# First layer's self-attention by pairs of heads: two heads' scores side by side in two row groups, eight steps, division one step later

## The chip, the cores and the metric

The kernel runs on one core of one Trainium2 chip. The metric is the device time of one execution in microseconds (us), the median of several. The core has a matrix engine (TensorE, PE in the profile), whose weight loads are shown apart (PEld), a vector engine (VectorE, DVE), an activation engine (ScalarE, ACT), GpSimd (POOL) and SyncE (SP), which issues most DMAs. Each engine runs its own list of instructions in order; semaphores tie the lists together. TensorE reads from SBUF (here one big tensor, `arena`) and writes to PSUM, which has eight banks of 128 partitions x 512 f32 words.

## The reference

Two decoder layers over 4 sequences of 512 tokens with 256 features. The first layer has a Mamba block with a grouped-query attention and a gated feed-forward inside it, a cross-attention with 16 heads, and a mixture of experts. The second has block-diagonal attention, cross-attention and another mixture of experts. The change touches only this part of the first layer:

```python
N_HEADS = 4
N_KV = 2
head_dim = D // N_HEADS          # 64
q = (xn @ q_w.T).reshape(B, L, N_HEADS, head_dim).transpose(0, 2, 1, 3)
k = (xn @ k_w.T).reshape(B, L, N_KV, head_dim).transpose(0, 2, 1, 3)
v = (xn @ v_w.T).reshape(B, L, N_KV, head_dim).transpose(0, 2, 1, 3)
k = jnp.repeat(k, hpg, axis=1)   # hpg = 2: heads 0, 1 use key head 0, heads 2, 3 key head 1
v = jnp.repeat(v, hpg, axis=1)
attn = jnp.einsum('bhqd,bhkd->bhqk', q, k) * scale
attn = jnp.where(causal[None, None], -jnp.inf, attn)
attn = jax.nn.softmax(attn, axis=-1)
out = jnp.einsum('bhqk,bhkd->bhqd', attn, v)
out = out.transpose(0, 2, 1, 3).reshape(B, L, D) @ o_w.T
```

## The kernel before, in words

The program is written out by hand, engine by engine: the order on each engine is the order of the source, and every wait names a semaphore and a count. The first layer runs one sequence after the other (the loop over `b`, four rounds). A round is: the selective scan, the output projection of the Mamba block, the self-attention, its output projection, the gated feed-forward, the cross-attention. TensorE takes part in all of them.

The stage that the change touches is the self-attention of a round. It has 16 units `u`, one for each block of 128 queries (`qc = u // 4`) and head (`h = u % 4`). Keys are causal, so block `qc` looks at `nk = 128, 256, 384 or 512` keys. All data are f32. The steps of a unit are:

- `scores(u)` on TensorE (L854, L856): queries x keys of one head into PSUM bank 4 or 5 (by turns). The contraction is over the 64 features of a head, so only 64 of the 128 rows of the array hold weights: rows 0 to 63 for heads 0 and 1, rows 64 to 127 for heads 2 and 3. Then one small bf16 matmul over all 128 rows (L856) adds the causal mask to the last 128 columns.
- `row_max(u)` on VectorE (L2007): minus the maximum of each row.
- the exponential on ScalarE (L1584), with the row sums, which it reads out in a second instruction (ACTIVATION_READ_ACCUMULATOR) before it signals `p_ready`.
- `transpose_p(u)` on TensorE (L863): `qc + 1` transposes into bank 6 or 7, and a copy of them to SBUF by VectorE (L2020).
- `weigh_v(u)` on TensorE (through the helper `acc`, L652, shape 128x64): transposed probabilities x values, into bank 2 or 3.
- after the fourth head of a block: VectorE inverts the four row sums (L2025) and multiplies (L2030, "the division"); TensorE transposes the result (`transpose_o`, L879), ScalarE drains it (L1576).

TensorE's list puts `scores(u + 1)` ahead of `transpose_p(u)`, and `weigh_v(u - 1)` behind it. Between them stand five tiles of the value projection for the cross-attention (`values_tile`, L652, shape 128x512, after the units in `XV_WHEN`); ScalarE drains them (L1571). The tiles go round through PSUM banks 0 and 1, in the order that `XV_AT` and `OT0_AT` number. VectorE's list has `row_max(u + 1)` ahead of the copy of unit `u`; its division of a block stands directly behind the copy of the block's last unit, and waits for that unit's `weigh_v`.

The cross-attention of the same kernel already computes two heads at once: in `xscores` (L938) a loop over two row groups issues one matmul with its weights in rows 0 to 63 and one with rows 64 to 127, next to each other, each 512 columns wide, into two banks.

Of the kernel before, what the change touches and what calls it, by code (L numbers as in the profile page):

```python
# [6 lines left out]
B, L, D = 4, 512, 256  # L7
P = 128
T = B * L
KD = D // P  # L10
NC = L // P
# [11 lines left out]
XV_WHEN, OT0_AT, XK = (1, 3, 5, 9, 13), (3, 5, 7, 8), ("xk_a", "xk_b")  # L23
XV_AT = [("att", i) for i in (0, 1, 2, 4, 6)] + [("xv", i) for i in range(3)]
# [124 lines left out]
def decoder_program(nc, A, out):  # L149
# [5 lines left out]
    with ctx:  # L155
# [48 lines left out]
        caus16 = take16(P)  # L204
# [35 lines left out]
        pr = [take(L) for _ in range(2)]  # L240
        ptb = [take(NC, P) for _ in range(2)]
# [15 lines left out]
        t2 = [take(2, L, at=squares_at + 2 * i * L) for i in range(TBUFS)]  # L257
        sums_at = squares_at + 2 * TBUFS * L
# [387 lines left out]
        def _(pe):  # L646
# [106 lines left out]
            for b in range(B):  # L753
# [94 lines left out]
                def scores(u):  # L848
                    qc, h = u // 4, u % 4
                    nk, g = (qc + 1) * P, h // 2  # L850
                    if u >= 2:
                        w(p_ready, u - 1)
                    s = bank[4 + u % 2]
                    mm(s[:, 0:nk], qT[64 * g:64 * g + 64, h % 2, qc * P:(qc + 1) * P],  # L854
                       kT[64 * g:64 * g + 64, 0:nk], start=True, stop=False)
                    mm(s[:, qc * P:nk], ident16, caus16, start=False, stop=True).then_inc(s_full.sem, 1)  # L856

                def transpose_p(u):
                    w(p_ready, u + 1)
                    if u >= 2:  # L860
                        w(pt_sb, u - 1)
                    for kc in range(u // 4 + 1):
                        r = transpose(bank[6 + u % 2][:, kc * P:(kc + 1) * P], pr[u % 2][:, kc * P:(kc + 1) * P], ident)  # L863
                    r.then_inc(pt_full.sem, 1)

                def weigh_v(u):
                    qc, h = u // 4, u % 4
                    w(pt_sb, u + 1)
                    if h == 0 and qc >= 2:
                        w(o_step, 2 * (qc - 1))  # L870
                    acc(bank[2 + qc % 2][:, 64 * h:64 * h + 64],
                        [(ptb[u % 2][:, kc, :], va[:, kc, 64 * (h // 2):64 * (h // 2) + 64]) for kc in range(qc + 1)])\
                        .then_inc(pv_done.sem, 1)
# [9 lines left out]
                for u in range(U0):  # L883
                    if u + 1 < U0:
                        scores(u + 1)
# [1768 lines left out]
```

## Time and profile before

| | |
|---|---|
| median of 3 runs | 2936.61 us (2935.52 to 2940.99) |
| the profiled execution | 2925.96 us, its span 2924.1 us |
| mean granted TensorE clock of it | 0.945 |
| TensorE busy | 2613.8 us (89% of the span) |
| VectorE busy | 1442.7 us (49%) |
| ScalarE busy | 1088.5 us (37%) |
| GpSimd busy | 681.2 us (23%) |

All durations below are from the profiled execution, which was 10.65 us faster than the median. In the rows, PE MATMUL is a matmul and PEld its weight load. An f32 matmul shows as two MATMUL and two LDWEIGHTS instructions. The ends of matmuls are modelled, and they overlap; what a matmul costs TensorE is read from one start to the next. A row of the timeline merges neighbours and names the first one's shape: the six matmuls at 622.60 are one value product of 64 columns (two) and a value tile of 512 columns (four).

### The profile page before, as it was taken

The numbers are of one execution on the slowest core, as the hardware profiler recorded it, in microseconds if no ns is written. First come the engines' busy times: TensorE is split into PE (matmuls) and PEld (weight loads), VectorE is DVE, ScalarE is ACT, GpSimd is POOL, SyncE is SP. The second block draws the span as 40 slices with busy tenths as digits, with TensorE's granted clock in tenths as the row PEclk, the third lists the DMA queues.
The fourth block names the chain that finished last, engine by engine and source line by source line (L and its number), as shares of the span: only waits on it lengthen the run. The fifth ranks groups of instructions, "written<-read, shape, count | busy, mean of one in ns | idle before, by whom it ended". The sixth has DMA issues, their size and how long they took to land. (4 is left out here: it accounts for less than half of the span.)

```text
span 2924.1 us, 40088 instructions
## 1 busy us (share of the span) xinstructions
PE 2613.8 (89%) x16441; PEld 1564.8 (54%) x16441; DVE 1442.7 (49%) x2107; ACT 1088.5 (37%) x1885; POOL 681.2 (23%) x364
## 2 busy tenths in 40 slices
PE   7679999989999999999949978999989998699997
PEld 4256533844266534754228855464554544477776
DVE  5566337932876347932821124555445554633432
ACT  3764234722564245622502213534335342011111
POOL 0256024900665034900720020000000000022222
PEclk9889999999999999999979987999999998699999
DMA  5550002100030002100039940010100102144442
GB/s 198 200 186 25 0 1 98 60 1 1 1 134 23 1 0 111 46 1 0 1 133 329 343 144 16 1 23 23 22 23 1 23 8 94 34 146 147 166 164 73
DMA packets 62126, 219.25 MB, mean 75 GB/s; under 512 B 12293, under 2 KB 28122, under 8 KB 45178
## 3 DMA queue, kind: packets, MB, share of 16 engines
q1 hardware_dynamic: 45802, 187.39, 17.7%
q0 software_dynamic: 9568, 18.75, 2.7%
q10 hardware_dynamic: 6576, 10.57, 1.0%
q8 instruction: 130, 2.13, 0.3%
q14 instruction: 50, 0.41, 0.0%
HBM read 172.50 MB, written 39.99 MB: 73 GB/s over the span
## 5 line engine op out<-in xcount | busy, mean ns | idle before, releaser
L652 PE MATMUL psum<-arena 128*128 128x256 f32 (+7 forms) x4224 | 1098.4, 411 | 66.4 <-ACT arena L1514 11.5
L652 PEld LDWEIGHTS psum<-arena 128*128 128x128 f32 (+1 forms) x4224 | 679.0, 196 | 434.9 <-issue 321.1
L2473 POOL TENSOR_TENSOR arena<-arena 128x1024 f32<-128x1024 f32 x128 | 299.5, 2372 | 98.4 <-DVE arena L1979 83.5
L1979 DVE TENSOR_TENSOR_SCAN arena<-arena,psum 128x512 f32<-128x512 f32 x256 | 290.8, 1200 | 22.4 <-PE psum L793 14.6
L793 PEld LDWEIGHTS psum<-arena 128*128 128x128 f32 x2048 | 236.6, 193 | 49.4 <-ACT arena L1544 40.3
L793 PE MATMUL psum<-arena 128*128 128x128 f32 x2048 | 249.0, 279 | 2.0 <-issue 1.9
L2508 POOL DMA_INDIRECT arena<-xn,arena x32 | 31.6, 987 | 859.3 <-DVE arena L2415 807.6
L2480 POOL TENSOR_TENSOR arena<-arena 128x1024 f32<-128x1024 f32 x32 | 75.9, 2373 | 653.0 <-ACT arena L1632 653.0
L2073 DVE SCALAR_TENSOR_TENSOR arena<-psum,arena 128x1024 f32<-128x1024 f32 x128 | 156.8, 1243 | 80.5 <-PE psum L938 80.1
L1632 ACT ACTIVATE arena<-arena 128x1024 f32<-128x1024 f32 x128 | 146.7, 1146 | 110.1 <-DVE arena L2073 109.9
L1811 ACT ACTIVATE arena<-psum 128x256 f32<-128x256 f32 x128 | 49.2, 384 | 322.1 <-PE psum L652 322.1
L1537 ACT ACTIVATE arena<-arena 128x512 f32<-128x512 f32 x256 | 163.0, 708 | 0.0
L1772 ACT ACTIVATE arena<-psum 128x1024 f32<-128x1024 f32 x128 | 128.7, 1023 | 67.5 <-PE psum L1266 64.4
L2484 POOL TENSOR_TENSOR arena<-arena 128x1024 f32<-128x1024 f32 x64 | 151.2, 2362 | 10.2 <-ACT arena L1632 1.3
L949 PE MATMUL psum<-arena 128*64 128x512 f32 x512 | 138.2, 617 | 15.5 <-ACT arena L1632 7.4
L1266 PE MATMUL psum<-arena 32*128 32x512 f32 x512 | 138.1, 652 | 8.6 <-ACT arena L1772 5.4
L938 PE MATMUL psum<-arena 64*128 64x512 f32 x512 | 142.5, 638 | 2.8 <-ACT arena L1610 2.8
L1241 PE MATMUL psum<-arena 32*128 32x512 f32 x512 | 138.8, 676 | 5.3 <-DVE arena L2271 5.3
L2057 DVE RECIPROCAL arena<-arena 128x256 f32<-128x256 f32 x64 | 110.9, 1743 | 46.2 <-ACT arena L1624 46.2
L2274 DVE TENSOR_REDUCE arena<-psum 128x2 f32<-128x1024 f32 x96 | 114.1, 1222 | 25.3 <-PE psum L1241 22.1
L1431 PE MATMUL psum<-arena 128*128 128x256 f32 x512 | 117.5, 382 | 0.0
L2438 DVE TENSOR_TENSOR arena<-arena,psum 128x256 f32<-128x256 f32 x128 | 53.1, 420 | 114.4 <-ACT arena L1811 112.8
(293 smaller groups left out, 2985.3 us busy)
## 6 DMA issues: line engine op xcount, KB each, us to landing
arena<-in_W SPq DMA_DIRECT2D x46, 1024.0 KB
arena<-c_rows SPq DMA_DIRECT2D x32, 512.0 KB, 3.9
arena<-in_Wg SPq DMA_DIRECT2D x16, 1024.0 KB, 4.9
arena<-in_Wu SPq DMA_DIRECT2D x16, 1024.0 KB, 7.6
arena<-in_Wd SPq DMA_DIRECT2D x16, 1024.0 KB, 10.0
arena<-in_xT SPq DMA_DIRECT2D x8, 512.0 KB, 5.9
zs_all<-arena SPq DMA_DIRECT2D x4, 1024.0 KB, 3.9
ut_all<-arena SPq DMA_DIRECT2D x4, 1024.0 KB, 8.8
```

The lines of the kernel that those rows point to most:

```text
L652: r = mm(dst, w, x, start=i == 0, stop=i == len(pairs) - 1)
L793: r = mm(bank[4 + c][:, q * P:(q + 1) * P], duT[:, q, c * P:(c + 1) * P], diag[n % 2][:, q, :], start=True, stop=True)
L938: i = mm(bank[2 + 2 * (u % SBUFS) + r], xkT[64 * r:64 * r + 64, hp, kc * P:(kc + 1) * P], xqT[64 * r:64 * r + 64, hp, :], start=True, stop ...
L949: i = mm(bank[0][64 * r:64 * r + 64, :], v1[:, kc, 2 * hp + r, :], t2[u % TBUFS][:, r, :], start=kc == 0, stop=kc == NC - 1)
L1241: r = mm(t[:, j - j0, :], q4[32 * j:32 * j + 32, g, qc * P:(qc + 1) * P], k4[32 * j:32 * j + 32, g, :], start=True, stop=True)
L1266: r = mm(bank[4 + 2 * ((i + g) % 2) + j % 2], k4[32 * j:32 * j + 32, g, kc * P:(kc + 1) * P], q4[32 * j:32 * j + 32, g, :], start=True, st ...
L1537: A_(dA[n % 2][:, c, :], dl[:, c, :], ACT.Exp, scale=aneg[:, c, n:n + 1]).then_inc(dA_ready.sem, 1)
L1632: A_(t2[u % TBUFS], rl[u % RBUFS], ACT.Square, scale=0.125, bias=vec[:, V_NB:V_NB + 1])\
L1979: V.tensor_tensor_scan(hs[n % 3][:, c, :], dA[n % 2][:, c, :], bank[4 + c], 0.0, ALU.mult, ALU.add)\
L2073: V.scalar_tensor_tensor(rl[u % RBUFS], t, minus_nb8, bound[:, kc, :].unsqueeze(1).broadcast_to([P, 2, L]), ALU.max, ALU.min).then_inc(rel ...
L2473: nc.gpsimd.tensor_tensor(h, h, c_all[:, n % CBUFS, :].unsqueeze(1).broadcast_to([P, 2, L]), ALU.mult)\
L2484: nc.gpsimd.tensor_tensor(t, t, t2[kc], ALU.add).then_inc(tsum_step.sem, 1)
```

## The change

The 16 units become 8 steps `i`. A step takes one block of queries (`qc = i // 2`) and two heads, `a` and `a + 2` with `a = i % 2`: one in rows 0 to 63 of the array, one in rows 64 to 127 (`g` = 0, 1). The two scores matmuls are issued next to each other, into banks 4 and 5, and then the two mask matmuls. There is one pair of score banks where before each unit had the other bank than its neighbour: `scores(i)` waits until both exponentials of step `i - 1` are done (`p_ready`, 2i). Row maxima, exponentials, transposes, copies and `weigh_v` are the same instructions in the same number, two at a time. VectorE's division of a block moves one step back: behind the copies of the first step of the next block. The value tiles stand in steps 0 to 4, and the order in banks 0 and 1 is numbered anew. The buffers `pr` and `ptb` become twice as large and share their place with `dl`, `duT` and `t2`, which are not in use in this stage.

```diff
-XV_WHEN, OT0_AT, XK = (1, 3, 5, 9, 13), (3, 5, 7, 8), ("xk_a", "xk_b")
-XV_AT = [("att", i) for i in (0, 1, 2, 4, 6)] + [("xv", i) for i in range(3)]
+OT0_AT, XK = (3, 6, 7, 8), ("xk_a", "xk_b")
+XV_AT = [("att", i) for i in (0, 1, 2, 4, 5)] + [("xv", i) for i in range(3)]
...
+        pr = [take(2, L, at=squares_at + 2 * i * L) for i in range(2)]
+        ptb = [take(2, NC, P, at=squares_at + (4 + 2 * i) * L) for i in range(2)]
...
-                def scores(u):
-                    qc, h = u // 4, u % 4
-                    nk, g = (qc + 1) * P, h // 2
-                    if u >= 2:
-                        w(p_ready, u - 1)
-                    s = bank[4 + u % 2]
-                    mm(s[:, 0:nk], qT[64 * g:64 * g + 64, h % 2, qc * P:(qc + 1) * P],
-                       kT[64 * g:64 * g + 64, 0:nk], start=True, stop=False)
-                    mm(s[:, qc * P:nk], ident16, caus16, start=False, stop=True).then_inc(s_full.sem, 1)
-
-                def transpose_p(u):
-                    w(p_ready, u + 1)
-                    if u >= 2:
-                        w(pt_sb, u - 1)
-                    for kc in range(u // 4 + 1):
-                        r = transpose(bank[6 + u % 2][:, kc * P:(kc + 1) * P], pr[u % 2][:, kc * P:(kc + 1) * P], ident)
-                    r.then_inc(pt_full.sem, 1)
-
-                def weigh_v(u):
-                    qc, h = u // 4, u % 4
-                    w(pt_sb, u + 1)
-                    if h == 0 and qc >= 2:
-                        w(o_step, 2 * (qc - 1))
-                    acc(bank[2 + qc % 2][:, 64 * h:64 * h + 64],
-                        [(ptb[u % 2][:, kc, :], va[:, kc, 64 * (h // 2):64 * (h // 2) + 64]) for kc in range(qc + 1)])\
-                        .then_inc(pv_done.sem, 1)
+                def scores(i):
+
+                    qc, a = i // 2, i % 2
+                    nk = (qc + 1) * P
+                    if i >= 1:
+                        w(p_ready, 2 * i)
+                    for g in range(2):
+                        mm(bank[4 + g][:, 0:nk], qT[64 * g:64 * g + 64, a, qc * P:(qc + 1) * P],
+                           kT[64 * g:64 * g + 64, 0:nk], start=True, stop=False)
+                    for g in range(2):
+                        mm(bank[4 + g][:, qc * P:nk], ident16, caus16, start=False, stop=True).then_inc(s_full.sem, 1)
+
+                def transpose_p(i):
+                    for g in range(2):
+                        w(p_ready, 2 * i + g + 1)
+                        if i >= 1:
+                            w(pt_sb, 2 * (i - 1) + g + 1)
+                        for kc in range(i // 2 + 1):
+                            r = transpose(bank[6 + g][:, kc * P:(kc + 1) * P], pr[i % 2][:, g, kc * P:(kc + 1) * P], ident)
+                        r.then_inc(pt_full.sem, 1)
+
+                def weigh_v(i):
+                    qc, a = i // 2, i % 2
+                    for g in range(2):
+                        h = a + 2 * g
+                        w(pt_sb, 2 * i + g + 1)
+                        if h == 0 and qc >= 2:
+                            w(o_step, 2 * (qc - 1))
+                        acc(bank[2 + qc % 2][:, 64 * h:64 * h + 64],
+                            [(ptb[i % 2][:, g, kc, :], va[:, kc, 64 * g:64 * g + 64]) for kc in range(qc + 1)])\
+                            .then_inc(pv_done.sem, 1)
...
                 scores(0)
-                for u in range(U0):
-                    if u + 1 < U0:
-                        scores(u + 1)
-                    transpose_p(u)
-                    if u >= 1:
-                        weigh_v(u - 1)
-                    if u % 4 == 2 and u >= 4:
-                        transpose_o(u // 4 - 1)
-                    if u in XV_WHEN:
-                        values_tile(XV_WHEN.index(u))
-                weigh_v(U0 - 1)
+                for i in range(U0 // 2):
+                    if i + 1 < U0 // 2:
+                        scores(i + 1)
+                    transpose_p(i)
+                    if i >= 1:
+                        weigh_v(i - 1)
+                    if i % 2 == 1 and i >= 3:
+                        transpose_o((i - 3) // 2)
+                    if i < 5:
+                        values_tile(i)
+                weigh_v(U0 // 2 - 1)
...
+                for i in range(U0 // 2):
+                    qc, nk = i // 2, (i // 2 + 1) * P
+                    for g in range(2):
+                        w(s_max, 2 * i + g + 1)
+                        if i >= 2:
+                            w(pt_full, 2 * (i - 2) + g + 1)
+                        h = i % 2 + 2 * g
+                        A_(pr[i % 2][:, g, 0:nk], bank[4 + g][:, 0:nk], ACT.Exp, bias=negm[:, g:g + 1],
+                           accum_out=rsum[:, qc, h:h + 1]).then_inc(p_ready.sem, 1)
+                    if i % 2 == 0 and i >= 4:
+                        drain_oT((i - 4) // 2)
+                    if 1 <= i < 6:
+                        drain_values(i - 1)
+                drain_oT(NC - 2)
...
+                def row_max(i):
+                    nk = (i // 2 + 1) * P
+                    for g in range(2):
+                        w(s_full, 2 * i + g + 1)
+                        if i >= 1:
+                            w(p_ready, 2 * (i - 1) + g + 1)
+                        V.reduce_max(negm[:, g:g + 1], bank[4 + g][:, 0:nk], AX.X, negate=True).then_inc(s_max.sem, 1)
+
+                def divide_o(qc):
+                    w(p_ready, 4 * (qc + 1))
+                    if qc >= 1:
+                        w(o_step, 2 * qc)
+                    V.reciprocal(rinv[:, 0:4], rsum[:, qc, 0:4]).then_inc(o_step.sem, 1)
+                    w(o_step, 2 * qc + 1)
+                    w(pv_done, 4 * (qc + 1))
+                    if qc >= 2:
+                        w(LA.drained, LA.upto("att", OT0_AT[qc - 2] + 1))
+                    V.tensor_tensor(o_nat[:, qc % 2, :].rearrange("p (h e) -> p h e", h=4),
+                                    bank[2 + qc % 2][:, 0:D].rearrange("p (h e) -> p h e", h=4),
+                                    rinv[:, 0:4].unsqueeze(2).broadcast_to([P, 4, 64]), ALU.mult)\
+                        .then_inc(o_step.sem, 1)
 
                 row_max(0)
...
+                for i in range(U0 // 2):
+                    qc = i // 2
+                    if i + 1 < U0 // 2:
+                        row_max(i + 1)
+                    for g in range(2):
+                        w(pt_full, 2 * i + g + 1)
+                        if i >= 2:
+                            w(pv_done, 2 * (i - 2) + g + 1)
+                        V.tensor_copy(ptb[i % 2][:, g, 0:qc + 1, :],
+                                      bank[6 + g][:, 0:(qc + 1) * P].rearrange("p (a b) -> p a b", b=P))\
+                            .then_inc(pt_sb.sem, 1)
+                    if i % 2 == 0 and i >= 2:
+                        divide_o(qc - 1)
+                divide_o(NC - 1)
```

On TensorE, the last block of queries (512 keys). L854, L856, L863, L879 are scores, mask, transposes of the probabilities and transposes of the output; their lines are L855, L858, L866, L884 in the changed kernel; L652 128x64 is `weigh_v`. Before, two units:

```order
L854 MATMUL psum<-arena 128x512
L856 MATMUL psum<-arena 128x128
L863 MATMUL psum<-arena 128x128 x3
L652 MATMUL psum<-arena 128x64 x3
L854 MATMUL psum<-arena 128x512
L856 MATMUL psum<-arena 128x128
L863 MATMUL psum<-arena 128x128 x4
L652 MATMUL psum<-arena 128x64 x3
```

and in the changed kernel, from the step that first computes such scores:

```order
L855 MATMUL psum<-arena 128x512 x2
L858 MATMUL psum<-arena 128x128 x2
L866 MATMUL psum<-arena 128x128 x6
L652 MATMUL psum<-arena 128x64 x6
L884 MATMUL psum<-arena 128x128 x2
L855 MATMUL psum<-arena 128x512 x2
L858 MATMUL psum<-arena 128x128 x2
L866 MATMUL psum<-arena 128x128 x8
L652 MATMUL psum<-arena 128x64 x6
```

The same matmuls now stand in twos: two scores, two masks, and then the transposes and the value products of two heads.

On VectorE, where the block with 256 keys ends. L2007 and L2020 are row maximum and copy, L2025 and L2030 the two instructions of the division; in the changed kernel L2018, L2043, L2024, L2029. Before:

```order
L2020 COPY arena<-psum 128x256
L2007 TENSOR_REDUCE arena<-psum 128x1
L2020 COPY arena<-psum 128x256
L2025 RECIPROCAL arena<-arena 128x4
L2030 TENSOR_TENSOR arena<-psum,arena 128x256
L2007 TENSOR_REDUCE arena<-psum 128x1
L2020 COPY arena<-psum 128x384
```

and now:

```order
L2043 COPY arena<-psum 128x256 x2
L2018 TENSOR_REDUCE arena<-psum 128x1 x2
L2043 COPY arena<-psum 128x384 x2
L2024 RECIPROCAL arena<-arena 128x4
L2029 TENSOR_TENSOR arena<-psum,arena 128x256
```

The division of that block stood right behind its last copy; it now stands behind the next block's first two row maxima and copies.

## Rows read from the trace of the kernel before

**Rows 1.** The page, busy time by engine: us (share of span) and instructions.

```profile
PE 2613.8 (89%) x16441; PEld 1564.8 (54%) x16441; DVE 1442.7 (49%) x2107; ACT 1088.5 (37%) x1885; POOL 681.2 (23%) x364
```

**Rows 2.** The four stages: length, busy PE, PEld, DVE, ACT, POOL, granted clock, DMA share.

```profile
294.55:338.49 43.94, 39.93 (x197) 23.79 (x197) 16.16 (x40) 14.58 (x42) 0.00 (x0) 0.96 0.00 0
619.97:662.29 42.32, 38.31 (x196) 22.92 (x197) 16.16 (x40) 14.58 (x42) 0.00 (x0) 1.00 0.00 1
946.60:990.49 43.89, 39.88 (x197) 23.79 (x197) 16.17 (x40) 14.53 (x42) 0.00 (x0) 0.96 0.00 1
1272.00:1314.26 42.26, 38.25 (x196) 22.86 (x196) 16.17 (x40) 14.53 (x42) 0.00 (x0) 1.00 0.00 1
```

**Rows 3.** Timeline, second round's stage begins: start, duration, engine, instructions, [idle before <-releaser].

```profile
619.97 0.49 PE L854 MATMUL psum<-arena 64*128 64x128 f32 x2 [0.69 <-ACT arena L1565]
...
620.39 0.23 PE L856 MATMUL psum<-arena 128*128 128x128 bf16 x1
...
620.96 0.23 PE L856 MATMUL psum<-arena 128*128 128x128 bf16 x1
...
621.59 0.36 ACT L1584 ACTIVATE arena<-psum,arena 128x128 f32<-128x128 f32 x1
...
621.74 0.33 PE L863 MATMUL psum<-arena 128*128 128x128 f32 x1 [0.55 <-ACT arena L1584]
621.84 0.20 ACT L1584 ACTIVATION_READ_ACCUMULATOR arena<-psum,arena 128x1 f32 x1
...
622.00 0.49 PE L854 MATMUL psum<-arena 64*128 64x128 f32 x2
...
622.60 2.11 PE L652 MATMUL psum<-arena 128*128 128x64 f32 x6
...
624.63 0.49 PE L854 MATMUL psum<-arena 64*128 64x128 f32 x2
```

**Rows 4.** Timeline, the division at the end of the 128-key block.

```profile
629.61 0.70 PE L854 MATMUL psum<-arena 64*128 64x256 f32 x2
629.79 0.43 DVE L2030 TENSOR_TENSOR arena<-psum,arena 128x256 f32<-128x256 f32 x1 [2.62 <-PE psum L652]
...
630.24 0.23 PE L856 MATMUL psum<-arena 128*128 128x128 bf16 x1
...
631.20 0.44 PE L863 MATMUL psum<-arena 128*128 128x128 f32 x2 [0.73 <-ACT arena L1584]
```

**Rows 5.** Timeline, the last unit of 512 keys and what follows it.

```profile
655.31 1.12 PE L854 MATMUL psum<-arena 64*128 64x512 f32 x2
...
656.36 0.23 PE L856 MATMUL psum<-arena 128*128 128x128 bf16 x1
...
656.43 0.61 PE L863 MATMUL psum<-arena 128*128 128x128 f32 x4
...
656.87 1.00 PE L652 MATMUL psum<-arena 128*128 128x64 f32 x8
...
657.71 0.39 PE L879 MATMUL psum<-arena 128*128 128x128 f32 x2
```

**Rows 6.** Timeline of TensorE in the cross-attention: pairs of heads.

```profile
423.99 1.13 PE L938 MATMUL psum<-arena 64*128 64x512 f32 x4
425.05 1.08 PE L949 MATMUL psum<-arena 128*64 128x512 f32 x4
```

**Rows 7.** Groups by line and form, whole execution: count, busy us, mean ns, idle before.

```profile
L863 PE MATMUL psum<-arena 128*128 128x128 f32 x160 | 29.9, 285 | 11.8 <-ACT arena L1584 11.8
...
L2007 DVE TENSOR_REDUCE arena<-psum 128x1 f32<-128x512 f32 x16 | 11.0, 686 | 18.3 <-PE psum L856 18.3
...
L1584 ACT ACTIVATE arena<-psum,arena 128x512 f32<-128x512 f32 x16 | 11.0, 688 | 33.8 <-DVE arena L2007 33.8
```

More of the change, by code:

```diff
@@ L239, in decoder_program @@
         qT, kT, va = take(KD, L), take(L), take(NC, P)
-        pr = [take(L) for _ in range(2)]
-        ptb = [take(NC, P) for _ in range(2)]
         negm, rsum, rinv = take(2), take(NC, LH), take(LH)
@@ L1577, in drain_oT @@
                         .then_inc(LA.drained.sem, 1)
-                for u in range(U0):
-                    nk = (u // 4 + 1) * P
-                    w(s_max, u + 1)
-                    if u >= 2:
-                        w(pt_full, u - 1)
-                    A_(pr[u % 2][:, 0:nk], bank[4 + u % 2][:, 0:nk], ACT.Exp, bias=negm[:, u % 2:u % 2 + 1],
-                       accum_out=rsum[:, u // 4, u % 4:u % 4 + 1]).then_inc(p_ready.sem, 1)
-                    if u - 2 in XV_WHEN:
-                        drain_values(XV_WHEN.index(u - 2))
-                    if u % 4 == 3 and u >= 4:
-                        drain_oT(u // 4 - 1)
+                for i in range(U0 // 2):
[12 more added lines that the diff above has]
+                drain_oT(NC - 2)
                 drain_oT(NC - 1)
```

28 lines of the change are left out of this document (removed).

## The prediction, made before the changed kernel had run

> **What bounds the kernel now.** I read the page first: TensorE is busy for 89% of the span, no other engine for half of it [rows 1]. That is an average, so I read the busy time of the four self-attention stages. Each lasts 42.3 or 43.9 us, and TensorE is busy for 38.3 to 39.9 of them. VectorE works for 16.2 us, ScalarE for 14.6, GpSimd not at all, and the DMA share is 0.00 [rows 2]. So TensorE's own list sets the length: its work, and some 4 us in which it waits for an exponential or a division. The reader is to see in the timeline that scores of 128, 256 and 512 keys cost 0.42, 0.63 and 1.05 us from their start to the mask's [rows 3, 4, 5], that TensorE waits at the transposes (L863) in a few units, and that the same kernel's cross-attention issues pairs of 64-row matmuls [rows 6].
>
> **Term A, scores side by side: minus 5.9 us a stage.** Width adds 0.21 us per 128 columns, so 384 keys cost 0.84. Four heads of each width cost 4 x (0.42 + 0.63 + 0.84 + 1.05) = 11.8 us a stage. In the cross-attention, four instructions of 512 columns in two row groups (two heads) go from 423.99 to 425.05, 1.06 us [rows 6]; two such instructions (one head) take 1.05 here [rows 5]. The second head is free there. The change makes the same pattern: weights at partitions 0 and 64, neighbours in the list, two banks. So eight pairs cost 5.9 us, and 5.9 are saved. The pair row is for 512 columns only; narrow pairs are not in these rows. At worst a pair costs what two heads cost (A is then 0). At best it costs nothing over one. I take the nearest row, full overlap. Between the ends, a surcharge of up to 0.2 us a pair (the part of each price that does not grow with width) would be 1.6 us a stage, and I keep it for the range.
>
> **Term B, the division one step later: minus 2.7 us a stage.** Before, VectorE's multiply of a block (L2030) waits for TensorE's last value product of the block, 2.62 us in the row, and the next row maximum is queued behind it. So the next exponential is late, and TensorE, which has issued the mask at 630.24, starts the transposes only at 631.20: 0.96 us, where the undisturbed distance is 0.07 (656.36 to 656.43) [rows 4, 5]. That is 0.89 us, of which the profile shows 0.73 as idle. The group of L863 shows 11.8 us of idle in all four stages [rows 7]. The starts of the stages account for 4 x 0.55 [rows 3]; the remaining 9.6 us lie at three block ends and the last unit of each stage. At three block ends a stage, 3 x 0.9 = 2.7 us. In the new order the two row maxima and copies of the next step stand ahead of the division. Its value products have then been issued before TensorE needs VectorE again, and the queue behind it (row maxima of the step after next) is for scores that TensorE issues only after a value tile or further value products. Ends of this term: 2.2 (the shown idle only) and 2.7. I take 2.7. The last division has nothing to hide behind in either order.
>
> **Term C, the pause at the start: plus 0.8 us a stage.** The second pair of scores waits for both exponentials of the first. The first one can't start earlier than now, since its table load comes first; the second one's read-out ends at 621.84 + 0.20 = 622.04. So the second pair starts at about 622.10. Before, TensorE had by 622.00 issued two scores and the first transpose (621.74, 0.26 us with the way to the next start) [rows 3]. The new list has at 622.10 only the two scores behind it: 0.36 us behind, and the 0.42 that term A credits for the first pair is not earned either. 0.8 in all.
>
> **Term D, switches of the array: minus 0.3 us a stage.** A mask matmul is followed by a scores matmul after 0.16 us (620.39 to 620.55), by a transpose after 0.07 [rows 3, 5]. Entering the 64-row form so costs 0.09, and it is entered 8 times instead of 16: 0.7 us. Against it stands the second mask in a row, which no row shows. If it costs 0.16 instead of 0.07, all 0.7 are lost again. So 0 to minus 0.7; I take minus 0.3. The Trainium skill (TensorEngine Tiling (Array Packing), Key Properties) says that a change of tiling mode drains TensorE. The trace agrees in kind: 0.21 us of each score's price do not grow with width. If leaving and entering both cost that much, as the rule by itself would have it, another 8 x 0.2 = 1.6 us a stage would go; the 0.16 us above speak against it, and the sum goes by the rows.
>
> **New waits, and what hides them.** There is one pair of score banks now, so each pair of scores waits for both exponentials of the pair before. That chain, at 512 keys: scores 1.05, first mask 0.23, two row maxima 2 x 0.69, the second exponential 0.69, its read-out 0.1, and the hand-overs 0.1: 3.55 us [rows 3, 5, 7]. Behind the waiting instruction stand the transposes of the step. TensorE's cover is what stands between two pairs. In the barest step (the first with 512 keys, without a value tile) these are scores 1.05, masks 0.2, six transposes 0.66, six value products 1.26, transposes of the output 0.3 (four transposes take 0.44, four value products 0.84 [rows 5]): 3.5 us. A tie, a wait of 0 to 0.1 us. In steps 1 to 4 a value tile adds 1.8 us (622.60 to 624.63 less one value product of 0.2 [rows 3]). With 384 keys that is 4.3 us against at most 3.35, even by the durations of 512 keys. In step 0 it is 2.6 against at most 2.9 by those durations. Without the cover, each step would cost TensorE about 2 us more (see the third rival). VectorE has two maxima and two copies a step, 4 x 0.69 = 2.8 us at most, and a division of 0.6 in every second one: 3.4, still under 3.5, but close. I take 0.1 us a stage for all new waits, within the rounding. ScalarE has two exponentials and a tile, 2.3 us. The tail (last copy, division, transposes of the output, drain) is the same chain as before. No DMA is issued or moved in the stage; the new places of `pr` and `ptb` add no wait.
>
> **Sum.** 5.9 + 2.7 - 0.8 + 0.3 - 0.1 = 8.0 us a stage, four stages: 32 us. What follows the stage is TensorE's work again, so nothing waits for another event there. The profiled execution took 2925.96 us and would take 2894. The median stands 10.65 us above it: 2936.61 - 32 = 2904.6, say 2904.5.
>
> **The clock.** Two of the four stages show a granted clock of 0.96 and last 1.6 us longer than the two at 1.00 [rows 2]: part of them ran at 1.2 instead of 2.4 GHz. The low stretch can follow the pause before and in the first units, and the changed kernel pauses longer there. All four low: plus 3.2 us. None: minus 3.2. I leave it at two.
>
> **Rivals.**
> - The pairs do not overlap (the second head's weight load or its f32 passes wait for the first's). Then A is gone, and C loses its 0.4: 2.7 - 0.4 + 0.3 = 2.6 us a stage, 10 us, 2926. For it: narrow pairs are not in the rows. Against it: the pair at 423.99. 4%.
> - Partial: the narrow pairs overlap in part and all four stages start low. 1.6 x 4 + 3.2 = 9.6 us of the 32 go, 2914. For it: the 0.2 us that does not shrink with width, and the longer pause. Against it: the pair row has the same constant part and hides it. 12%.
> - Slower, by lockstep: VectorE's row maxima, copies and divisions of two heads come so late that TensorE runs each step from its scores to its last value product before the next. At 512 keys a step would then last the chain of 3.55 plus second transposes 0.44, copy 0.69, value products 0.84 and hand-overs: 5.7 us, against 3.5 with cover, so 2.2 us of waiting. Narrower steps have less, some 1.6 on the mean; over seven steps 11 us, against 8.0 gained: 3 us a stage, 12 in all, 2949. It decides from 8.0 / 7 = 1.1 us of waiting a step. For it: one set of banks, and VectorE's 3.4 us in a step of 3.5. Against it: the list puts finished work of the last step behind each pair of scores, and VectorE is busy for only 16.2 of 42.3 us. 3%. The Trainium skill (TensorEngine Tiling (Array Packing), PSUM Bottleneck) warns of this: tiling speeds up TensorE but not the emptying of PSUM. The 16.2 us of VectorE and 14.6 of ScalarE against a stage of 34 say that there is room.
> - The gain doesn't reach the end, because something after the stage is due at a fixed time: 2936. The DMA share of 0.00 and the idle GpSimd speak against it. 2%.
> - More than forecast: entering and leaving the 64-row form both cost 0.2 us, as the drain rule has it: 6 us more, 2898. 7%.
>
> The forecast itself has 72%, with 2899 to 2910. A difference under 0.2% (6 us) can't be told from none. Faster by more: the forecast, the partial one, the drain rule and most of the first rival, 0.94. Slower 0.03, same 0.03. The range 2897 to 2917 adds to the forecast both clock cases, the surcharge of the narrow pairs, the drain rule's side and 2 us for the spread of the median; it leaves out the first, third and fourth rival and the edges of the others.
>
> **What the profile after would show.** If A is right, each scores row holds four instructions and its distance to the mask is 0.42, 0.63, 0.84, 1.05 us, and a stage lasts 34 to 36 us at 33 or less of busy TensorE. If B is right, no transposes wait 0.7 us for an exponential after a block's end. If C is right, the second pair starts 2.1 us after the first. Waits of over 0.3 us before scores in steps 2 to 7, or VectorE idle nowhere, would show lockstep. Distances of over 0.6 and about 2 us at 128 and 512 keys would show that the pairs run one after the other. A stage that shrinks by 8 us with a round that does not would show that the gain is lost later.

## The result, and the profile after

The changed kernel took 2893.16 us (median of 4, 2890.55 to 2895.95) against 2936.07 us: a ratio of 0.985 (0.9833 to 0.9868), 43 us faster. That is below the low end of my range (2897). Timed again beside other kernels it took 2897.95 us (0.9885, 0.9869 to 0.9902) and 2892.94 us (0.9865, 0.9843 to 0.9887), while the kernel before took 2933 to 2935 us. The first of these two lies inside my range, the other below it. So the change gains between 34 and 43 us, depending on the executions compared; I had forecast 32.

The profiled execution has a span of 2888.7 us, 35.4 less than the one of before. The page's row of busy time, against [rows 1]:

```profile
PE 2585.6 (90%) x16440; PEld 1555.3 (54%) x16441; DVE 1440.2 (50%) x2107; ACT 1089.0 (38%) x1885; POOL 681.3 (24%) x364
```

The four stages of self-attention (length, busy PE, PEld, DVE, ACT, POOL, granted clock, DMA share), against [rows 2]:

```profile
296.69:331.69 35.00, 32.50 (x197) 20.98 (x197) 15.51 (x40) 14.70 (x42) 0.00 (x0) 0.95 0.00 0
614.29:649.27 34.98, 32.48 (x196) 21.11 (x196) 15.51 (x40) 14.70 (x42) 0.00 (x0) 0.95 0.00 1
931.83:966.77 34.94, 32.44 (x197) 21.11 (x197) 15.52 (x40) 14.69 (x42) 0.00 (x0) 0.95 0.01 1
1249.27:1284.20 34.93, 32.43 (x196) 21.10 (x196) 15.52 (x40) 14.69 (x42) 0.00 (x0) 0.95 0.00 1
```

They are 139.9 us together, where they were 172.4: 32.6 us less, 8.1 a stage, of 8.0 forecast. All four now have a stretch at the lower clock, where before two of four had one. The other 2.8 us of the 35.4 lie outside the stages.

The start of the second round's stage in the timeline, against [rows 3]:

```profile
614.29 0.49 PE L855 MATMUL psum<-arena 64*128 64x128 f32 x4 [0.69 <-ACT arena L1570]
...
614.72 0.28 PE L858 MATMUL psum<-arena 128*128 128x128 bf16 x2
...
616.16 0.20 ACT L1591 ACTIVATION_READ_ACCUMULATOR arena<-psum,arena 128x1 f32 x1
...
616.41 0.80 PE L855 MATMUL psum<-arena 64*128 64x128 f32 x4 [1.41 <-ACT arena L1591]
...
617.14 0.40 PE L858 MATMUL psum<-arena 128*128 128x128 bf16 x2
```

The first pair of scores is four instructions, and its mask follows after 0.43 us, as it did for one head. Then TensorE waits until the second exponential is read out (616.36), 2.12 us after the stage's start: term C as forecast. The mask of the second pair comes after 0.73 us instead of 0.43: from 616.41 to 619.84 the granted clock is 0.50, that is 1.2 GHz.

The last block of queries, against [rows 5]:

```profile
635.95 1.13 PE L855 MATMUL psum<-arena 64*128 64x512 f32 x4
...
637.01 0.28 PE L858 MATMUL psum<-arena 128*128 128x128 bf16 x2
...
637.13 0.82 PE L866 MATMUL psum<-arena 128*128 128x128 f32 x6
...
639.08 0.39 PE L884 MATMUL psum<-arena 128*128 128x128 f32 x2
...
639.50 0.30 PEld L855 LDWEIGHTS psum<-arena 64*128 64x128 f32 x4 [0.27 <-ACT arena L1591]
...
639.50 1.13 PE L855 MATMUL psum<-arena 64*128 64x512 f32 x4
...
642.87 1.23 PE L866 MATMUL psum<-arena 128*128 128x128 f32 x8
...
645.66 0.39 PE L884 MATMUL psum<-arena 128*128 128x128 f32 x2
...
645.89 1.90 PE L652 MATMUL psum<-arena 128*128 128x64 f32 x16
```

Two heads' scores of 512 keys take 1.06 us to their mask, where one head took 1.05. The step lasts 3.55 us (635.95 to 639.50); the chain and the cover were a tie at 3.5. The row of the matmul shows no wait, but the row of its weight load does: it is released by the exponential, whose read-out ends at 639.45. The output's transposes in front of it (639.08) take 0.42 us to the scores, where they take 0.31 when nothing has to be waited for (1278.10 to 1278.41 in the run with the later division, shown further down). So this step waits 0.1 us, in every stage. The last transposes follow the value products at 642.87 with no wait, and the output's transposes are followed by other work after 0.23 us.

The groups of the whole execution (count, busy us, mean ns, idle before and its releaser), against [rows 7]:

```profile
L866 PE MATMUL psum<-arena 128*128 128x128 f32 x160 | 24.6, 282 | 0.0
...
L884 PE MATMUL psum<-arena 128*128 128x128 f32 x32 | 6.4, 282 | 2.3 <-DVE arena L2029 2.3
...
L855 PE MATMUL psum<-arena 64*128 64x128 f32 x32 | 5.0, 402 | 8.4 <-ACT arena L1591 5.6 <-ACT arena L1570 2.8
```

No transposes of probabilities wait for an exponential any more; they had 11.8 us of it. The longer pause before the second pair is new (5.6 us in the four stages, 1.41 each). The last division still costs 0.58 us a stage.

### The profile page after: what moved, and what is told of

It reads as the page before. It is cut to its first block and busy times, and to the rows that moved or that the text cites. A ratio compares the mean times of both kernels' runs of the same rounds, so it can differ in the third digit from the quotient of the medians.

```text
span 2888.7 us, 40083 instructions
## 1 busy us (share of the span) xinstructions
PE 2585.6 (90%) x16440; PEld 1555.3 (54%) x16441; DVE 1440.2 (50%) x2107; ACT 1089.0 (38%) x1885; POOL 681.3 (24%) x364
## 5 line engine op out<-in xcount | busy, mean ns | idle before, releaser
L652 PE MATMUL psum<-arena 128*128 128x256 f32 (+7 forms) x4224 | 1093.5, 411 | 64.4 <-ACT arena L1519 11.5
L652 PEld LDWEIGHTS psum<-arena 128*128 128x128 f32 (+1 forms) x4224 | 676.1, 195 | 432.6 <-issue 320.8
L2523 POOL DMA_INDIRECT arena<-xn,arena x32 | 31.6, 987 | 857.1 <-DVE arena L2430 805.7
L954 PE MATMUL psum<-arena 128*64 128x512 f32 x512 | 138.2, 617 | 15.5 <-ACT arena L1640 7.4
```

The costliest lines, as they stand in the source:

```text
L652: r = mm(dst, w, x, start=i == 0, stop=i == len(pairs) - 1)
L954: i = mm(bank[0][64 * r:64 * r + 64, :], v1[:, kc, 2 * hp + r, :], t2[u % TBUFS][:, r, :], start=kc == 0, stop=kc == NC - 1)
```

## The experiments

The first job asked how much of the 43 us is scatter, and priced the two halves of the change apart.

**The kernel before, again** (no edit).

> The kernel before, unchanged, for its profile on the same chip as the other runs. The changed kernel's profiled execution was 35.4 us shorter than the one of before, its median 43 us. Theory 1 (the executions of before scatter, and its one profiled execution, 2925.96 us, was a short one): this profile lasts 2930 to 2941 us, and the four self-attention stages in it last 42.3 or 43.9 us as before; the extra time lies outside them. Theory 2 (the change gains more than its profile shows): this profile lasts about 2926 us again and the timed executions 2936. Ratio to before 1.00.

The median of 11 executions is 2936.55 us, from 2931.19 to 2939.60 (1.0012, 1.0 to 1.0023). The kernel before, run beside it, ranged from 2926.68 to 2943.49. The profile has a span of 2934.5 us: 10.4 us more than the one I had read. Three of its stages last 43.9 us, one 42.3. Two stretches outside the stages, in the profile I had read and then in this one:

```profile
338.49:619.97 281.48, 269.76 (x1707) 139.44 (x1707) 173.49 (x164) 130.42 (x217) 131.80 (x56) 0.99 0.11 41
1314.26:2924.10 1609.84, 1414.69 (x9007) 913.36 (x9007) 683.12 (x1228) 478.06 (x786) 184.54 (x143) 0.93 0.26 87
```

```profile
338.92:622.58 283.66, 271.96 (x1706) 139.92 (x1706) 173.50 (x164) 130.42 (x217) 131.88 (x56) 0.98 0.11 41
1318.25:2934.50 1616.25, 1414.69 (x9006) 911.12 (x9007) 682.62 (x1228) 477.75 (x786) 184.60 (x143) 0.93 0.26 87
```

The same instructions took 2.2 and 6.4 us longer. The first is a matter of the clock (0.98 for 0.99). The second has the same rounded clock; most of its difference is one wait near the start of the second layer, in the first profile and in the second:

```profile
1732.80 2.07 PE L1069 MATMUL psum<-arena 128*128 128x128 f32 x8 [0.57 <-DVE arena L2166]
```

```profile
1747.19 2.08 PE L1069 MATMUL psum<-arena 128*128 128x128 f32 x8 [5.95 <-DVE arena L2166]
```

TensorE waits there for a chain that begins with a square root on ScalarE (L1685), and in the second profile this instruction starts 5 us later although its input is there; the profile names no instruction that it waited for. The same wait lasts 0.57, 4.86 and 0.57 us in three profiles of the changed kernel (at 1698.96, 1704.02 and 1698.50 us). So it comes and goes from execution to execution of one kernel, far from the edited code. In the changed kernel the same two stretches:

```profile
331.69:614.29 282.60, 270.86 (x1706) 139.88 (x1706) 173.51 (x164) 130.45 (x217) 131.83 (x56) 0.99 0.11 41
1284.20:2888.70 1604.50, 1410.47 (x9006) 912.26 (x9007) 683.09 (x1228) 478.10 (x786) 184.56 (x143) 0.93 0.26 87
```

Theory 1 holds: the one profiled execution of before was a short one. The times of single executions go with their mean granted clock: of 60 executions of the kernel before in the three jobs (2924.95 to 2943.49 us), the eight with a clock of 0.945 or more took 2928.6 us on the mean, the twelve with 0.940 or less 2937.8.

**The changed kernel, again** (no edit).

> The changed kernel, unchanged, timed in the same rounds. Theory (stages alone): a ratio of 0.988 to 0.990 (33 to 36 us), stages of 35.0 us in the profile. Rival (8 us more are gained somewhere outside the stages): 0.985 again.

2897.95 us, a ratio of 0.9885 (0.9869 to 0.9902): this fits the theory and not the rival. The stages last 34.99, 34.97, 34.94 and 34.94 us in a span of 2894.8.

**The masks between the scores.**

```diff
                     for g in range(2):
                         mm(bank[4 + g][:, 0:nk], ...)
-                    for g in range(2):
                         mm(bank[4 + g][:, qc * P:nk], ident16, caus16, ...)
```

> The changed kernel with each head's mask matmul directly behind its scores matmul, so that the two 64-row matmuls are no longer neighbours. If the neighbours' overlap is term A: scores to mask stays 0.42 to 1.06 us but occurs twice a step, the stage grows by 5.9 + 0.5 (switches) - 0.4 (the pause at the start hides the first) = 6.0 us to 41, the whole by 24 us over the changed kernel, about 2916. Rival (the gain comes from the order of the steps and the later division, the overlap is small): under 8 us more than the changed kernel.

2929.54 us (0.9985, 0.997 to 1.0), 31.6 over the changed kernel in the same job, where 24 were expected. The third round's stage ran at the full clock:

```profile
944.54:983.76 39.22, 37.27 (x196) 22.82 (x196) 16.27 (x40) 15.59 (x42) 0.00 (x0) 1.00 0.00 1
```

```profile
968.43 1.12 PE L855 MATMUL psum<-arena 64*128 64x512 f32 x2
969.49 0.23 PE L857 MATMUL psum<-arena 128*128 128x128 bf16 x1
969.65 1.12 PE L855 MATMUL psum<-arena 64*128 64x512 f32 x2
970.70 0.23 PE L857 MATMUL psum<-arena 128*128 128x128 bf16 x1
```

Each head's scores now take 1.05 or 1.06 us by themselves. Where TensorE runs at the full clock a stage of the changed kernel lasts 33.4 us (shown below), so the overlap is worth 5.8 to 5.9 us a stage, 23.4 in all. The two profiles of the job differ by 33.2 us: 23.3 of them in the stages (163.1 against 139.8), 9.9 outside (2764.9 against 2755.0). The stages bear out the expectation; what exceeds it lies outside them, in an execution with a mean granted clock of 0.938 against 0.944.

**Only the division later, in the kernel before.**

```diff
-                    if u % 4 == 3:
-                        (reciprocal and multiply of block qc)
+                    if u % 4 == 0 and u >= 4:
+                        divide_o(qc - 1)
+                divide_o(NC - 1)
```

> The kernel before with nothing but the division moved one unit later on VectorE (behind the first row maximum and copy of the next block). Term B: the 0.73 us waits at the transposes of the second unit of a block are gone, the stage is 2.7 us shorter (39.6 where it was 42.3), four stages 10.8 us, 2925 if before is 2936. Rival (the wait only moves to a later matmul): no change, 2936.

2917.65 us (0.9947, 0.9932 to 0.9962): 15.7 us less than before, where 10.8 were expected. Two of its stages ran at the full clock; one of them, and the group of the transposes:

```profile
942.92:982.55 39.63, 37.87 (x196) 22.75 (x196) 16.38 (x40) 14.69 (x42) 0.00 (x0) 1.00 0.00 1
```

```profile
L863 PE MATMUL psum<-arena 128*128 128x128 f32 x160 | 29.5, 282 | 2.8 <-ACT arena L1584 2.8
```

42.3 to 39.63: term B is 2.7 us a stage, as forecast. Of the 11.8 us of idle 2.8 are left: the start, 0.55 a stage, and 0.16 at the last unit.

The second job put the division back, filled the pause, and tried the order inside a step.

**The division back in its place, with pairs.**

```diff
-                    if i % 2 == 0 and i >= 2:
-                        divide_o(qc - 1)
-                divide_o(NC - 1)
+                    if i % 2 == 1:
+                        divide_o(qc)
```

> The changed kernel with VectorE's division put back directly behind the copies of a block's last step. Term B from the other side. Where a value tile follows (blocks of 128 and 256 keys) it hides most of the wait, 0 to 0.6 us each; where none follows (the block of 384 keys) the row maxima of the last step stand behind a division that waits for eight transposes and six value products, so some 2.5 us before the last transposes. Stage 35.0 + 3.3 = 38.3 us, +13 us over the changed kernel (about 2911 beside 2898). Rival (with pairs the later division no longer matters): stage 35.0, no difference.

2931.01 us (0.9992, 0.9983 to 1.0002), 33 us over the changed kernel as the first job had timed it, instead of 13. The waits are those of the expectation (308.50, 317.74, 327.27), but behind the longest one the clock falls:

```profile
295.19:337.53 42.34, 36.64 (x197) 24.76 (x197) 15.43 (x40) 14.47 (x42) 0.00 (x0) 0.85 0.00 1
```

```profile
308.50 0.92 PE L855 MATMUL psum<-arena 64*128 64x384 f32 x4 [0.20 <-ACT arena L1591]
...
317.74 1.13 PE L855 MATMUL psum<-arena 64*128 64x512 f32 x4 [0.55 <-ACT arena L1591]
...
327.27 1.48 PE L866 MATMUL psum<-arena 128*128 128x128 f32 x8 [2.46 <-DVE arena L2043]
328.54 3.51 PE L652 MATMUL psum<-arena 128*128 128x64 f32 x16
```

16 instructions of value products took 3.51 us, where they take 1.90 at the full clock. From 328.1 us to the end of the stage the granted clock is 0.50. The mean of the stage is 0.85, and the stage lasts 42.3 us. In the other three rounds it lasts 40.4 us, and there the clock is full at the start, behind the same pause of 1.41 us:

```profile
622.98 0.49 PE L855 MATMUL psum<-arena 64*128 64x128 f32 x4 [1.41 <-ACT arena L1591]
```

So in these rounds 3.2 us of new waits cost 7 us over the 33.4 that a stage takes at the full clock. With pairs and the early division the whole gain is lost in the total. In the stages it is not lost quite: they take 163.5 us together (172.4 and 174.1 before), but the rest takes 2763.9 (2751.7 and 2760.4 before).

**A value tile in the pause.**

```diff
+                values_tile(0)
                 for i in range(U0 // 2):
                     ...
-                    if i < 5:
-                        values_tile(i)
+                    if i < 4:
+                        values_tile(i + 1)
```

(with the drains and the order in banks 0 and 1 moved alike)

> The changed kernel with its value tiles one place earlier: the first stands between the first and the second pair of scores, where TensorE waits 1.4 us (term C). If the pause is a cost of its own: it vanishes, a wait of 0.3 to 0.6 us comes up before the scores of step 6, which has lost its cover, net 1.0 us a stage. If the pause is also what lowers the granted clock to 0.5 behind it (a low stretch stands there in all four stages of the changed kernel): the low stretch goes too, another 1.6 us a stage. 35.0 to 34.0 without, 32.4 with: 4 or 10 us over the four stages, 2894 or 2888 beside 2898.

2895.57 us (0.9872, 0.9855 to 0.9889). A stage, and its start and the new wait:

```profile
610.56:642.88 32.32, 30.87 (x197) 20.24 (x197) 15.52 (x40) 14.68 (x42) 0.00 (x0) 1.00 0.01 1
```

```profile
611.11 1.93 PE L652 MATMUL psum<-arena 128*128 128x512 f32 x4
612.98 0.49 PE L855 MATMUL psum<-arena 64*128 64x128 f32 x4
...
629.55 1.13 PE L855 MATMUL psum<-arena 64*128 64x512 f32 x4 [0.36 <-ACT arena L1592]
```

The stage lasts 32.3 us, all at the full clock: the second theory. In all, though, the time is only 2.4 us less than that of the changed kernel in the job before, where 10 were expected; outside the stages this execution has 2764.6 us where that one had 2755.0.

**Tiles at start and tail.** As the one before, with the last tile behind the last transposes of the output (`transpose_o(NC - 1)`, `values_tile(4)`, then `act_has("att", 8)`).

> As the one before, and the last of the five value tiles stands behind the last transposes of the output, where TensorE waits 0.5 us for the drain (the output projection then waits for the drain of that transpose only). 0.5 us less there, 0.4 more before the scores of step 5, which loses its cover: 0 to 0.3 us a stage better than the one before, 0 to 1 us in all.

2890.14 us (0.9859, 0.984 to 0.9879), 5.4 us less than the one before, where 0 to 1 were expected. The two intervals overlap, so the timing does not tell them apart; the stage, shown with the repetition below, is 0.2 us shorter, as expected.

**Heads alternate inside a step.**

```diff
-                    transpose_p(i)
-                    if i >= 1:
-                        weigh_v(i - 1)
+                    for g in range(2):
+                        transpose_p(i, g)
+                        if i >= 1:
+                            weigh_v(i - 1, g)
```

> The changed kernel with transposes and value products alternating head by head, as before the change, instead of two heads' transposes and then two heads' products. If each hand-over between groups of matmuls costs TensorE 0.05 us by itself (the trace shows 1.2 us a stage that I did not forecast, with about half as many such groups), seven steps get two more each: plus 0.7 us a stage, plus 3 us in all. Rival (the 1.2 us come from waits for copies): the copies have less time in this order, so more than 1 us a stage, shown as idle before the products.

2899.36 us (0.988, 0.986 to 0.9901), no difference that the timing tells; the stage is 0.4 us shorter than that of the changed kernel, not longer:

```profile
611.90:646.50 34.60, 32.05 (x196) 20.75 (x196) 15.62 (x40) 14.70 (x42) 0.00 (x0) 0.95 0.00 1
```

The third job set the clock apart from the waiting, and compared the best orders in the same rounds.

**The changed kernel, a third time.**

> The changed kernel, timed beside the three others of this job. With the stages alone at work, a ratio of 0.987 to 0.989; stages of 35.0 us with a low stretch of the clock in each.

2892.94 us (0.9865, 0.9843 to 0.9887), a little under what the stages alone would give. The stages last 34.9 to 35.0 us, with a low stretch in each, as expected.

**Matmuls in the pause that nobody reads.**

```diff
                 scores(0)
+                mm(bank[1], ident, const[:, 0:L], start=True, stop=True)
+                mm(bank[1][:, 0:2 * P], ident, const[:, 0:2 * P], start=True, stop=True)
```

> The changed kernel with two more f32 matmuls (512 and 256 columns, 1.3 us) that nobody reads, between the first and the second pair of scores, where TensorE waits 1.4 us. The wait for the exponentials stays. If the idle time there is what lowers the clock: no low stretch in the stages, 33.4 us instead of 35.0 although TensorE has more to do. If the low stretch comes from elsewhere (the wait before the first scores, say): 35.0 to 35.2 us and the low stretch stays. In all, 6 us less than the changed kernel by the first if nothing is given back outside the stages; the version with the value tile in the same place lost 1.6 us a stage of low clock and gained only 2.4 us in all, with 10 us more outside the stages, so I expect 0 to 3 us less.

2897.43 us (0.9877, 0.9855 to 0.9898), 4.5 us more than the changed kernel in the same job, within the intervals, where 0 to 3 less were expected. The second round's stage, the stretch behind it, the one behind the fourth, and the start:

```profile
610.56:643.93 33.37, 32.22 (x201) 20.84 (x201) 15.53 (x40) 14.71 (x42) 0.00 (x0) 1.00 0.01 1
643.93:928.15 284.22, 272.50 (x1707) 140.44 (x1708) 173.54 (x164) 130.44 (x217) 131.89 (x56) 0.98 0.11 41
1279.02:2895.00 1615.98, 1418.52 (x9007) 916.52 (x9007) 683.13 (x1228) 478.04 (x786) 184.61 (x143) 0.92 0.26 87
```

```profile
611.11 1.07 PE L888 MATMUL psum<-arena 128*128 128x512 f32 x2
...
612.68 0.49 PE L855 MATMUL psum<-arena 64*128 64x128 f32 x4
```

The second pair still starts 2.12 us after the first. But no stage has a low stretch, and each lasts 33.37 us instead of 34.95: with the pause filled the low stretch is gone, in all four stages here as in those of the runs with a value tile there, and with it 1.6 us a stage. That is shown. The pause alone does not bring it, though. Three stages of the run with the division back have the same pause of 1.41 us and no low stretch at the start; the kernel before has low stretches behind a pause of 0.55 us. What goes with it is the clock ahead of the stage: in the nine profiles whose pause is not filled, 27 of 36 stages have the low stretch, and there the mean granted clock from 32 to 20 us ahead of the stage was 0.57 or 0.72; the nine without it had 0.86.

The unread matmuls brought nothing in all. The low stretches came up elsewhere: two of the three stretches between the stages last 284.1 to 284.2 us at a clock of 0.98, where the changed kernel has 282.5 at 0.99. The one behind the last stage has 1615.98 us at 0.92, where the changed kernel's had 1604.50, 1610.57 and 1608.01 at 0.93. The mean granted clock of the execution is 0.941, although its stages are at the full clock, against 0.944 in each of the three. Why the clock falls there, the runs don't show.

**Tiles at start and tail, again.**

> The version with value tiles at the start and at the tail, again, to compare it with the changed kernel in the same rounds: 5 to 8 us less than it (a ratio of 0.985 to 0.986 to before).

2888.45 us (0.9854, 0.983 to 0.9879), 4.5 us under the changed kernel in the same job, just short of the 5 to 8 expected, with overlapping intervals.

```profile
609.16:641.26 32.10, 30.78 (x197) 20.43 (x198) 15.53 (x40) 14.07 (x41) 0.00 (x0) 1.00 0.00 1
```

**The same with heads alternating.**

> That version with transposes and value products alternating head by head. Without a low stretch in the stage the row distances tell whether hand-overs between groups cost anything: by the theory of a cost per hand-over 32.1 + 0.7 = 32.8 us a stage. The run with alternating heads in the changed kernel showed 34.6 instead of 35.0, so the rival is that they cost nothing and the stage stays at 32.1, or 31.9.

2882.16 us of 5 (2880.84 to 2884.79; 0.9827, 0.981 to 0.9845), 10.8 us under the changed kernel, whose fastest was 2890.25. Its slowest execution is faster than the changed kernel's fastest. The stage:

```profile
609.13:640.95 31.82, 30.35 (x197) 20.18 (x198) 15.62 (x40) 14.08 (x41) 0.00 (x0) 1.00 0.01 1
```

31.8 us at the full clock: alternating costs nothing, the theory of a cost per hand-over between full-array matmuls has fallen. It gains 0.3 us a stage; why the time of the whole fell by more, 6 us, is open.

## Why the prediction was right or wrong

| term, us a stage | forecast | measured at the full clock |
|---|---|---|
| A, scores side by side | 5.9 | 5.84: scores to mask 11.78 before, 5.94 in the run with the unread matmuls |
| B, division later | 2.7 | 2.68: 42.31 to 39.63 |
| C, pause at the start | -0.8 | -0.9: a pause of 1.57 us (614.72 to 616.41 less the masks' 0.12) for 0.71 (620.96 to 621.74 less 0.07) |
| new waits | -0.1 | -0.1: 0.42 us for 0.31 in the barest step |
| D, switches and the rest | 0.3 | 1.4: what is left of 42.31 - 33.37 = 8.94 |
| sum | 8.0 | 8.94 |

- **Term A** was right in mechanism and size, for narrow pairs too. The first rival fell, and so did the partial overlap in the second: 128 keys take 0.43 us, 512 take 1.06. The second's other half, a low stretch in all four stages, came.
- **Term B** was right, and so was the reason.
- **Term C** was right (0.86 measured for 0.8). It stays in the changed kernel and is what the best version takes out.
- **The tie in the barest step** was right: 3.55 us, set by the chain, with the forecast wait of 0.1 us. The lockstep rival fell. The Trainium skill's warning (TensorEngine Tiling (Array Packing), PSUM Bottleneck) did not come true in this order of instructions: VectorE's 15.5 us are spread over a stage of 35. But how near it is shows in the run with the division back.
- **Term D was mis-sized.** "So 0 to minus 0.7; I take minus 0.3" measured 1.4. I had priced the entry into the 64-row form only behind a mask (0.09). It is also entered from value products and from the output's transposes. The run with the later division shows both prices:

```profile
1277.70 0.56 PE L652 MATMUL psum<-arena 128*128 128x64 f32 x4
1278.10 0.39 PE L879 MATMUL psum<-arena 128*128 128x128 f32 x2
1278.41 0.91 PE L854 MATMUL psum<-arena 64*128 64x384 f32 x2
...
1279.55 0.56 PE L652 MATMUL psum<-arena 128*128 128x64 f32 x4
1280.03 0.91 PE L854 MATMUL psum<-arena 64*128 64x384 f32 x2
```

Four instructions of value products take 0.40 us when transposes follow (1277.70) and 0.48 when scores follow (1279.55); the output's transposes take 0.31 before scores (1278.10), 0.23 before a value product in the changed kernel (645.66). So an entry costs 0.08 us there too, and eight entries are gone: 0.6 to 0.7 us. I had also left out the last unit, where before the transposes started 0.55 us behind those of the output (0.16 of it shown as idle); in the changed kernel 0.23: another 0.3. The masks bring 0.2, since the second of two in a row costs 0.05 us (637.01 to 637.13 is 0.12, one mask 0.07). The last 0.2 or so I can't put down to any row. The 1.6 us more of the Trainium skill's drain rule (TensorEngine Tiling (Array Packing), Key Properties) did not come: the entries cost 0.08 to 0.09, not 0.2.
- **The clock**: "I leave it at two". It was all four, in each of three profiles: 3.2 us of the 3.8 (4 x 0.94) by which a stage at the full clock beat the forecast were lost again. That is why the profiled stages gave 32.6 us, near the forecast, by two errors that cancel: luck. The prediction gave the longer pause as a reason for more low stretches. Filling the pause does remove them, but its length is not shown to be what made them four: the second profile of before has three of four with the short pause.
- **The step that failed**, and put the measured time outside the range, stands behind the stages: the whole was to shrink by what the stages gain and by nothing else, "so nothing waits for another event there", and the range had only "2 us for the spread of the median". The stages explain 32.6 to 34.2 us of the gain (by either profile of before), as forecast. But the median fell by 43, and by 35 and 42 in the two later timings. All 60 executions of before in the three later jobs have a mean of 2933.9 us, the 12 of the changed kernel in all its timings one of 2894.9: 39.0 us less. So 5 to 6 us were gained outside the stages, which the prediction put at nothing, and some 4 us of the first 43 are scatter: the three medians of the changed kernel alone (2893.16, 2897.95, 2892.94) lie 5 us apart.
- **The profiled execution as a base** was a bad one: "The median stands 10.65 us above it". I took this distance for a constant. A second profile of before is 10.4 us longer, and its executions range over 17 us; the changed kernel's first median stood 2.6 us above its profiled execution. The addition itself did no harm, since 2925.96 - 32 + 10.65 is the median of before less 32; but it hid how far single executions scatter.
- **What is beyond the stages** is in the profiles 2751.7 and 2760.4 us for before, 2748.9, 2755.0 and 2750.3 for the changed kernel: 4.7 us less on the mean. One part is the wait of 0.57 or some 5 us at the start of the second layer, which both kernels have in either length. Another is the granted clock. Whether the 5 us belong to the change or to scatter the runs don't settle: their cause is open.

## What to carry to other kernels

Two matmuls of 64 rows each that are neighbours in TensorE's list, in different row groups and banks, cost what one costs, at 128 columns as at 512; one full-array matmul between them undoes it. When a step shrinks this way, look at what VectorE has queued ahead of the next step's input: here the division had to move as well, and without it the total showed no gain (0.9992). Before forecasting an absolute time from one profile, ask how far single executions of that kernel scatter.

## What the runs showed of the hardware that I had not expected

- A wait of TensorE can cost more than it lasts: in all twelve profiled stages of the changed kernel 1.4 us of idle time were followed by a low stretch that cost another 1.6 us, and matmuls that nobody reads took it away (34.95 to 33.37 us). In three stages of another run the same pause was followed by the full clock. The wait of 2.46 us was followed by products at 3.51 us for 1.90.
- A gain of clock in one place need not show in the total: with 1.6 us a stage won back by unread matmuls, the rest of the program took 2761.5 us, where it took 2748.9 to 2755.0 in the changed kernel, and the mean granted clock of the execution was 0.941 for 0.944.
- Executions of one kernel differ by a wait that stands far from the edited code: 0.57 or about 5 us before the same eight matmuls, in both kernels.
